# VectorE takes the low parts of the token tiles a unit earlier, the doubled weight scans move from units 1 to 6 to units 8 to 13, and the steps of a top value lie two units apart instead of three

## What is computed

```
x = x + einsum('bct,bcd->bdt', x, weights[subjects])            # layer 0
q = rmsnorm(x @ Wq.T) * q_norm_w ; k = rmsnorm(x @ Wk.T) * k_norm_w ; v = x @ Wv.T
q, k = rope(q, pos), rope(k, pos)                               # 32 query heads, 8 key heads, D = 128
keys, values = cached pages of the sequence (512) + the 32 new ones, masked by length
o = softmax(q @ keys.T / sqrt(128)) @ values
x = x + o @ Wo.T
```

## Time and profile before

| | us |
|---|---|
| median of 3 runs | 1014.4 |
| lowest, highest | 1013.04, 1017.41 |
| the profiled execution, its own time | 1013.84 |
| its span, first to last instruction | 1012.0 |
| TensorE busy | 967.1 (96%) |
| VectorE busy | 818.9 (81%) |
| ScalarE busy | 736.2 (73%) |
| GpSimd busy | 539.9 (53%) |

### The profile page before, as it was taken

One profiled execution on the slowest core, in us unless ns is written; L12 is line 12 of the kernel. 1 busy time (PEld: TensorE's weight loads), 2 busy tenths in 40 slices (PEclk: granted clock), 3 DMA queues, 4 the chain that ended last, 5 costly groups with the idle time before them and its releaser, 6 DMA issues.

```text
span 1012.0 us, 24821 instructions
## 1 busy us (share of the span) xinstructions
PE 967.1 (96%) x8123; PEld 802.1 (79%) x8123; DVE 818.9 (81%) x1752; ACT 736.2 (73%) x2007; POOL 539.9 (53%) x709
## 2 busy tenths in 40 slices
PE   6899999999889988899999999999999999989998
PEld 4678888887678777778788888888888888878885
DVE  7889999999997698878878777777787787777770
ACT  5898999988775687767767676676776676766660
POOL 5565665566882167546554554455545544544440
PEclk9999999999999999999999999999999999999999
DMA  5799999989989889999999999989998998999940
GB/s 196 289 314 336 326 390 362 387 277 392 387 319 308 315 308 337 347 240 264 275 305 259 279 313 284 296 274 285 313 259 279 306 300 248 318 290 277 262 125 11
DMA packets 249904, 294.89 MB, mean 291 GB/s; under 512 B 79025, under 2 KB 206513, under 8 KB 247217
## 3 DMA queue, kind: packets, MB, share of 16 engines
q1 hardware_dynamic: 231088, 226.07, 75.0%
q0 software_dynamic: 18688, 67.25, 17.7%
HBM read 231.77 MB, written 46.27 MB: 275 GB/s over the span
## 4 chain that ended last, share of the span: by engine, by line
PE 65%; DVE 15%; issue 6%; ACT 6%; POOL 4%; DMA 3%; SPq 1%; DVEq 0%; ACTq 0%; POOLq 0%
PE ps_y L1489 15%; PE ps_o L1564 13%; PE ps_proj L1489 12%; PE ps_s L1527 7%; PE ps_s L1531 6%; PE ps_t L1538 6%; DVE rot L1361 2%; PE ps_rt L1659 2%; DVE probs L1228 2%; DVE stage L1371 1%; DVE rot L1353 1%; DVE c_stage L1385 1%; PE ps_t L1546 1%; ACT probs L1008 1%; PE ps_o L1576 1%
## 5 line engine op out<-in xcount | busy, mean ns | idle before, releaser
L934 POOL TENSOR_SCALAR probs<-probs,recip 128x544 f32<-128x544 f32 (+1 forms) x256 | 161.5, 631 | 298.3 <-DVE recip L1236 291.3
L1008 ACT ACTIVATE probs<-probs,neg_max 128x544 f32<-128x544 f32 x256 | 190.9, 746 | 150.8 <-DVE neg_max L1228 147.2
L1228 DVE CUSTOM_DVE_ANT_0 probs<-ps_s,mask,row_scale 128x544 f32<-128x544 f32 x256 | 200.5, 783 | 68.0 <-PE ps_s L1531 64.7
L1564 PE MATMUL ps_o<-pt,vs 128*128 128x128 f16 x3072 | 213.3, 219 | 1.9 <-DMA vs<-v_pages,v_row 1.9
L1564 PEld LDWEIGHTS ps_o<-pt,vs 128*128 128x128 f16 x3072 | 192.7, 98 | 16.5 <-DMA vs<-v_pages,v_row 2.4
L887 POOL TENSOR_TENSOR roped<-rot 128x256 f32<-128x256 f32 x160 | 145.2, 929 | 80.8 <-DVE rot L1353 77.6
L1248 DVE SCALAR_TENSOR_TENSOR pt<-ps_t,pt 128x512 f16<-128x512 f32 x190 | 130.0, 684 | 49.0 <-ACT pt L1014 48.9
L1489 PE MATMUL ps_proj<-wt_hi,x0t_hi 128*128 128x512 f32 x384 | 159.0, 415 | 5.9 <-DVE x0t_lo L1186 5.7
L1489 PE MATMUL ps_y<-wo,ot_hi 128*128 128x512 f16 x512 | 153.5, 381 | 2.6 <-DVE ot_lo L1260 2.6
L1489 PE MATMUL ps_proj<-wt_hi,x0t_lo 128*128 128x512 f32 x384 | 150.7, 394 | 0.0
L1489 PE MATMUL ps_proj<-wt_lo,x0t_hi 128*128 128x512 f32 x384 | 149.8, 391 | 0.0
(11 more groups left out here) (155 smaller groups left out, 1653.4 us busy)
## 6 DMA issues: line engine op xcount, KB each, us to landing
kt<-k_pages_t SPq DMA_DIRECT2D x512, 128.0 KB
c_nat<-in_L_cond_k_cache SPq DMA_DIRECT2D x32, 512.0 KB, 6.0
q_t<-stage SPq DMA_DIRECT2D x64, 256.0 KB, 7.3
c_nat<-in_L_cond_v_cache SPq DMA_DIRECT2D x32, 512.0 KB, 6.6
qt<-q_t SPq DMA_DIRECT2D x32, 512.0 KB, 3.7
w_nat<-in_L_cond_Wq SPq DMA_DIRECT2D x8, 1024.0 KB, 7.9
k_pages_t<-c_stage SPq DMA_DIRECT2D x16, 512.0 KB, 5.1
c_nat<-in_L_cond_Wo SPq DMA_DIRECT2D x16, 512.0 KB, 7.4
```

What stands on the lines that cost most here:

```text
L934: pool.tensor_scalar(part, part, col(recip, i), 1.0, ALU.mult, ALU.mult).then_inc(p_norm, 1)
L1008: act.activation(pr, pr, ACT.Exp, bias=col(neg_max, i), scale=-1.0, accum_out=col(row_sum, i)).then_inc(a_exp, 1)
L1228: dve.tensor_tensor_reduce(out=probs_of(i), in0=ps_s[:, score_cols(i):score_cols(i) + KEYS], in1=mask[(i // HK) % 2][:, mask_at(i):mask_at ...
L1564: ins = pe.matmul(ps_o[n % 2][:, jl * P:(jl + 1) * P], v[:, part, :], pt[pt_slot(i)][:, NCH * half + c, :], start=jl == 1 and c == 0 and k ...
```

## The change

On VectorE `x_low(2)` stands ahead of the loop, `l0_weights` and `l0_add` are one tile further on at the head of a unit, and `x_low(g + 3)` stands behind the low part of `ps_rt` in unit g. The tasks lie one a unit in units 1 to 7, two a unit in units 8 to 13, and from unit 14 on where they lay before. K_BOUND goes from 11 to 13, W_BOUND and V_BOUND stay, TOP_STEP goes from 3 to 2. So the key tops are reduced in unit 13 (was 11), turned in 15 (was 14) and broadcast in 17 (as before); those of the values are turned in 49 (was 50) and broadcast in 51 (was 53), those of Wo in 82 (was 83) and 84 (was 86). No instruction is added or removed.

```diff
-    TOP_STEP = 3
-    K_BOUND, V_BOUND, W_BOUND = 11, 47, 80
+    TOP_STEP = 2
+    K_BOUND, V_BOUND, W_BOUND = 13, 47, 80
...
-    PAIRS = 6
+    PAIRS, PAIRS_AT = 6, 8
...
-        TASK_IN[TASK_AT + t // 2 if t < 2 * PAIRS else TASK_AT + t - PAIRS].append(t)
+        alone = PAIRS_AT - TASK_AT
+        paired = min(max(0, t - alone), 2 * PAIRS)
+        TASK_IN[TASK_AT + t - (paired + 1) // 2].append(t)
...
+            x_low(2)
 
             for u in range(NU):
                 c, g = units[u]
-                if c == 0:
-                    if 1 <= g and g + 1 < NG:
-                        x_low(g + 1)
-                    if 1 <= g and g + 3 < NG:
-                        l0_weights(g + 3)
-                    if 1 <= g and g + 2 < NG:
-                        l0_add(g + 2)
+                if c == 0 and g + 4 < NG:
+                    l0_weights(g + 4)
+                if c == 0 and g + 3 < NG:
+                    l0_add(g + 3)
...
                                       ).then_inc(v_rtlo, 1)
+                if c == 0 and g + 3 < NG:
+                    x_low(g + 3)
                 if sum_in(u) is not None:
```

## The result

The changed kernel takes 1028.72 us (1027.87 to 1030.44) against 1014.4, a ratio of 1.0141 with a 95% interval of 1.0124 to 1.0157: 14.3 us slower. Forecast were 1023.4 us and a range from 1015.5 to 1028. The profiled execution's span went from 1012.0 to 1026.9 us, by 14.9. Where it went is read in the order of the prediction, first the timeline of TensorE in the changed kernel (start, duration, engine, line, instruction, [idle before, ended by]); its lines stand two further down than those of before.

A forecast was written before the change was run, and what follows sets the result against it. Bound: phase 1's front, where TensorE waits for others, carried to the end. Start of unit 16 +9.25, clock +0.8, recovery -0.4 sum to +9.6 us on 1013.84: 1023.4 us, range 1015.5 to 1028.

The forecast's parts named there:

- Unit 2 and the ladder to unit 7: TensorE's units 2 to 7 start earlier, unit 2 at 25.85 us; the gain reaches 4.35 us at unit 7.
- Unit 8: TensorE stands 3.2 us for weight chunk 1's last `w_low`; unit 8 starts at 58.0, leaving 0.3 us of the gain.
- The same could happen in unit 8, and is hidden by the wait for loads.: TensorE's clock could also halve in unit 8, but the later wait for loads would cover it: no cost.
- The load wait: ScalarE waits 5.8 us (bounds 0 and 7) for load 12, queued behind the `x_d` store; case chance 0.60.
- What is left when the loads are in time: Rival: without late loads, unit 16 starts +3.3 us later; +3 to +4.5 us in all, 1017.5 us, chance 0.22.
- The clock behind the tops: TensorE's clock halves after its wait for the key tops ahead of unit 16: 0.8 us, between 0 and 1.6.
- What comes back: Between units 15 and 25 TensorE's waits for VectorE, some 0.4 to 0.7 us, disappear: -0.4 us.
- The step of two: Key tops, reduced behind unit 13's page rows, hold TensorE ahead of unit 16; nothing at the values and Wo.
- After unit 24: What phase 1 has lost by unit 24 is carried to the end one for one; nothing further added.
- not slower: Rival: unit 8 starts at 54 to 56, keeping 1 to 3 us of the gain; 1010.5 to 1013 us, chance 0.10.

The follow-up runs named there:

- warm_8: Changed kernel plus 14 matmuls on constant data, result unread, ahead of unit 8: 1026.67 us, ratio 1.0116.
- tasks_only: Kernel before with tasks doubled in units 8 to 13, K_BOUND 13 and TOP_STEP 2, VectorE's order unchanged: 1026.55 us, ratio 1.0105.
- store_later: Changed kernel with the 2048 KB store of `x_d` in SyncE's unit 14 instead of 8: 1024.1 us, ratio 1.0090.
- tops_only: Kernel before with only K_BOUND 13 and TOP_STEP 2: 1016.42 us, ratio 1.0011.
- spread_store: Kernel before with `x_low(2)` ahead of the loop, doubled units 1, 2, 3, 7, 9, 11, `x_d` store in unit 14: 1014.84 us, ratio 0.9999.
- three_undone: Changed kernel with the `x_d` store in unit 14, 14 filler matmuls ahead of unit 8, and K_BOUND 12: 1019.21 us, ratio 1.0043.
- combined: Kernel before with `x_low(2)` ahead of the loop, doubled units 8 to 13, `x_d` store in unit 14, K_BOUND 12, TOP_STEP 2: 1018.29 us, ratio 1.0031.
- the first tile alone: Kernel before with only `x_low(2)` moved ahead of the loop: 1014.1 us, ratio 0.9986.
- order_only: Kernel before with only VectorE's new order, tasks and tops unchanged: 1025.92 us, ratio 1.0113.
- tops_in_12: Changed kernel with K_BOUND 12 instead of 13, key tops reduced ahead of the page rows: 1026.67 us, ratio 1.0118.
- sums_ahead: Kernel before with `x_low(2)` ahead of the loop, `l0_weights` and `l0_add` one tile further on, other `x_low` unmoved: 1031.85 us, ratio 1.0172.

## Why the prediction was wrong in size and right in direction

Slower was the forecast, and the mechanisms named for it are the ones in the trace. The time lies 0.7 us above the range, though, and 5.3 above the number. Point by point:

- *Unit 2 and the ladder to unit 7*: right. Predicted 31.55, 45.9 and 50.7 for units 3, 6 and 7, measured 31.93, 46.35 and 51.22.
- *Unit 8*: predicted 58.0 after a stand of 3.2 us, measured 58.76 after 3.37. Right; the last `w_low` of chunk 1 starts at 57.87, where it was 57.33.
- ***"The same could happen in unit 8, and is hidden by the wait for loads."* This step failed.** The wait for loads isn't a fixed date behind which the clock can hide: loads 11 and 12 are issued only when tasks 7 and 8 are scanned, one on ScalarE behind unit 8's squares, the other on VectorE behind unit 8's rotation, which waits for these squares. TensorE took 4.44 us from the start of unit 8 to its transposes (58.76 to 63.20) where warm_8 took 2.86. Load 11 went out at 66.09, in warm_8 at 64.47; load 12 at 68.05, in warm_8 at 67.03, and it landed at 79.71, in warm_8 at 78.44. So 1.3 of the 1.6 us came through, to the tops and to T24. The term put at nothing is 1.3 us.
- ***The load wait*, right in kind, mis-sized.** The tasks_only and store_later runs show the kind. But load 12 landed at 79.71, not at 75.8, and ScalarE stood 7.07 us, not 5.8 and a little more than the upper bound of 7. Of these 3.9 us 0.8 is the later start of unit 8 and 1.3 the half clock. The last 1.8 is the queue: the load was 11.66 us on its way, not 10.4 (the microsecond of latency in that figure stands in no row), and I had the engines moving 393 GB/s from 60 us on, where the window of 60 to 65 us shows 207 and the store went out at 62.02, not 60.5. From the landing to unit 16 it took 16.7 us where I had 17.65, 0.9 less. So T16 is 96.46, against 93.45: +12.25 in place of +9.25, and 3.9 - 0.9 gives these 3.0.
- *What is left when the loads are in time*: priced too low. The rival had T16 at 87.55, +3.3; store_later, with waits for loads of at most 1.5 us, has 91.21, +7.0. Three things make up about that difference: unit 8 starts at 59.11, not 58.0, its half clock is 1.6 us, and ScalarE still stands 1.46 us for load 12.
- *The clock behind the tops*: predicted 0.8 between 0 and 1.6. From the start of unit 16 to its transposes pass 4.36 us (96.46 to 100.82), before 2.74: it was the upper bound, 1.6. The half clock of 85 to 90 us, behind the 4.33 us wait, cost nothing that shows: the chain runs over ScalarE and VectorE there.
- *What comes back*: -0.4 predicted, nothing measured. T24 is +13.9, which is 12.25 and 1.6. I had VectorE ahead of TensorE from unit 16 on; the chain runs over VectorE's rotations and conversions from 109 to 127 us, as it did before from 95 to 113.
- *The step of two*: right; tops_only shows +1.1, and nothing at the values and Wo.
- *After unit 24*: predicted nothing, measured 1.0 us in the profiled execution, 0.3 by the first score product (354.70 for 340.52) and 0.7 in phase 2. I didn't find one cause for that; the waits of phase 2 have the same lines and nearly the same sums in both.

The sum from the measured terms: 9.6 + 3.0 (load and unit 8) + 0.8 (clock at unit 16) + 0.4 (nothing back) = 13.8, and 13.9 is measured.

Two further things the prediction had only as one number. It treated the order and the tasks as a joint ladder; the runs say that each by itself costs about 11 us, for different reasons. And "not slower" was tied to an earlier unit 8; spread_store has unit 8 at 55.66, 2.6 us sooner, and isn't faster. An early unit 8 is not enough: ScalarE and its loads must keep the lead to VectorE's rotation 12, from which VectorE has no gap.

What stays open: of the last +3.7 us of three_undone, combined (old order, same doubled units) has +2.0, which leaves about 1.7 us to the order; that is a difference of two profiled executions, and the two kernels differ in the fillers as well.

## What to carry to other kernels

Ask of each wait that you call hidden what *starts* the work it hides behind: if the cover is a transfer issued only when a buffer is freed by the very engines that are late, a delay isn't hidden but added. On an in-order engine, moving an instruction ahead of its producer's date puts the wait on everything queued behind it, loads that are issued on its completion included; check the producer's date at every unit, and not only at the first, where the move looks free (here the first tile alone was worth 1.4 us, the whole order cost 11.5). And don't double the pace of work that is fed by a queue in the same stretch in which that queue takes a large store; moving the store away took the longest waits out, but not all (3.25 us in combined).

## What the runs showed of the hardware

- A load of 512 KB issued behind a store of 2048 KB, a load of 1024 KB and a store of q on the same queue landed 11.66 us after its issue; the load of the earlier trace rows, as far behind, 11.9. Without the store ahead of it, in store_later, it was 6.49. SyncE's instruction for such a load itself lasted up to 3.0 us in that stretch (0.33 at the shortest), so that its next ones are issued late too (in warm_8 up to 2.7 us, and load 12 goes out 2.56 us behind load 11).
- TensorE's granted clock fell to the 1.2 GHz level behind waits of 3.37, 4.33 and 2.83 us in the changed kernel and behind 2.83 in the one before, and in order_only also behind 2.36 and 1.88. It stayed 1.00 behind waits of 2.48 to 2.52 in combined, tops_in_12 and three_undone, and behind one of 2.78 at 32.91 in sums_ahead. So the length of the last wait alone doesn't tell. The half clock made units 8 and 16 of the changed kernel 1.6 us longer each, and unit 14 2.2 us, there off the chain. Fourteen matmuls on constant data kept it at 1.00 across the wait ahead of unit 8.
